# Dense hop products with their operands swapped, float32r hop tables in two parts, and a reload without a split, in a two-layer graph kernel

## What is computed

```python
h = jnp.maximum(_layernorm(x, axis=-1), 0.0)
m_data, m_ctrl = h[src] @ W_data.T + b_data, h[src] @ W_control.T + b_control
msg = jnp.where((edge_types == 0)[:, None], m_data, m_ctrl)
x = x + relu(segment_sum(msg, dst) + (h @ W_self.T + b_self))
h = jnp.maximum(_layernorm(x, axis=-1), 0.0)
norm = deg_inv_sqrt[row] * deg_inv_sqrt[col]
y, out = h, h
for _ in range(2):
    y = segment_sum(y[row] * norm[:, None], col)
    out = out + y
x = x + out / 3
```

## Time and profile before

| | before |
|---|---|
| median of three runs | 3998.82 us |
| lowest, highest | 3994.66, 3999.19 us |
| span of the profiled execution (first to last instruction) | 3997.9 us |
| granted TensorE clock, mean over the span | 0.945 of 2.4 GHz |
| PE busy | 3405.9 us (85%) |
| PE weight loads busy | 2729.2 us (68%) |
| POOL busy | 2879.8 us (72%) |
| ACT busy | 2329.7 us (58%) |
| DVE busy | 2186.3 us (55%) |
| HBM traffic | 424.48 MB read, 142.99 MB written |

### The profile page before, as it was taken

How to read it: one execution, slowest core, us unless ns; L and a number is a source line. 1 busy time by engine, 2 the same in 40 slices (tenths; PEclk the granted TensorE clock), 3 DMA queues, 4 the chain that set the end, 5 groups by cost and what they waited for, 6 DMA issues and landing times.

```text
span 3997.9 us, 62254 instructions
## 1 busy us (share of the span) xinstructions
PE 3405.9 (85%) x23420; PEld 2729.2 (68%) x23420; DVE 2186.3 (55%) x3333; ACT 2329.7 (58%) x3075; POOL 2879.8 (72%) x3058
## 2 busy tenths in 40 slices
PE   7666777777777787777777899999998899999999
PEld 4344444444444444444444799999998899999999
DVE  7523888888888888888888422222222222222222
ACT  4001444444444444444444688888887788888887
POOL 2677777777777777777777577777776477777775
PEclk9788998999999999999999999999999999999999
DMA  6222333333333334333333566666666666666665
GB/s 194 85 61 61 109 119 121 113 109 110 126 109 110 114 110 128 110 109 125 110 115 112 170 179 187 192 192 187 189 189 184 179 179 176 187 182 181 179 184 145
DMA packets 367268, 571.77 MB, mean 143 GB/s; under 512 B 66678, under 2 KB 308225, under 8 KB 359283
## 3 DMA queue, kind: packets, MB, share of 16 engines
q1 hardware_dynamic: 270435, 370.74, 29.6%
q0 software_dynamic: 95664, 196.60, 19.2%
q10 hardware_dynamic: 864, 0.39, 0.0%
HBM read 424.48 MB, written 142.99 MB: 142 GB/s over the span
## 4 chain that ended last, share of the span: by engine, by line
PE 44%; POOL 38%; issue 13%; DVE 2%; DMA 2%; ACT 1%; SPq 0%; DVEq 0%; POOLq 0%; ACTq 0%
POOL rows L874 38%; PE wide L1175 34%; PE sums_bank L1091 7%; PE wide L1056 1%; ACT strip_ring L1011 1%; DMA stage<-hop_table 1%; DMA rows<-typed_table,index 0%; PE turned_bank L1126 0%; DVE big L1214 0%; DVE rows L1254 0%; DVE stage L1512 0%; POOL stage L914 0%; PE wide L1135 0%; DMA stage<-strips 0%; DMA big<-in_x 0%
## 5 line engine op out<-in xcount | busy, mean ns | idle before, releaser
L874 POOL DMA_INDIRECT rows<-typed_table,index x1661 | 1589.0, 957 | 506.0 <-issue 505.0
L874 POOL DMA_INDIRECT rows<-hop_table,index x1306 | 1251.9, 959 | 481.4 <-issue 394.9
L1011 ACT CAST strip_ring<-stage 128x1792 fp32r<-128x1792 uint8 x840 | 1409.2, 1687 | 285.3 <-PE wide L1175 279.2
L1175 PE MATMUL wide<-table_parts,strip_ring 128*128 128x256 f32 x11760 | 1461.0, 285 | 35.7 <-ACT strip_ring L1011 35.7
L1175 PEld LDWEIGHTS wide<-table_parts,strip_ring 128*128 128x128 f32 x11760 | 1431.3, 193 | 38.0 <-ACT strip_ring L1011 17.5
L1002 ACT CAST stage<-wide 128x392 uint8<-128x392 f32 x1920 | 790.3, 502 | 983.9 <-PE wide L1135 982.6
L1126 PE MATMUL turned_bank<-all_twos 128*128 128x512 bf16 x3328 | 1112.0, 394 | 0.0
L1091 PE MATMUL sums_bank<-rows,hot 128*128 128x129 f32 (+1 forms) x5934 | 801.2, 292 | 287.0 <-DMA rows<-typed_table,index 272.6
L1091 PEld LDWEIGHTS sums_bank<-rows,hot 128*128 128x128 f32 x5934 | 764.4, 206 | 337.8 <-issue 304.0
L1512 DVE TENSOR_TENSOR stage<-count_up,stage 128x1568 bf16<-128x1568 f32 x480 | 855.4, 1782 | 0.0
L1135 PE MATMUL wide<-stage 128*128 128x392 bf16 x1920 | 652.6, 340 | 221.8 <-DVE stage L1512 220.0
(11 more groups left out here) (141 smaller groups left out, 669.5 us busy)
## 6 DMA issues: line engine op xcount, KB each, us to landing
stage<-strips SPq DMA_DIRECT2D x840, 224.0 KB
strips<-stage SPq DMA_DIRECT2D x60, 1568.0 KB
rows<-typed_table,index POOLq DMA_INDIRECT x1661
rows<-hop_table,index POOLq DMA_INDIRECT x1306
resid<-xin SPq DMA_DIRECT2D x50, 256.0 KB, 3.0
hop_table<-scaled SPq DMA_DIRECT2D x50, 256.0 KB, 3.8
xin<-resid SPq DMA_DIRECT2D x50, 256.0 KB
typed_table<-rows SPq DMA_DIRECT2D x49, 256.0 KB, 2.1
```

Of the source, the lines that this page charges most:

```text
L874: pool.indirect_dma_start(out=rows[:, o % RING, c, 0:P], out_offset=None, in_=tables[k], in_offset=bass.IndirectOffsetOnAxis(ap=index[:, c ...
L1011: act.copy(strip_ring[:, number % STRIP_RING], counts_ring[place]).then_inc(strip_cast, 1)
L1175: last = pe.matmul(wide[:, nth % 4, 0:PARTS * P], strip_ring[:, number % STRIP_RING, b - first, :], table_parts[:, b, :, :].rearrange("p n ...
```

## The change

The parts:

- **Dense product.** The table part of a block becomes the stationary operand, and the counts of four tiles (a whole batch) the moving one, 512 columns. A step is now 4 blocks x 4 tiles; the product comes out transposed (features by nodes), is copied from PSUM in one piece per batch (`read_batch`) and turned back by four transposes (`turn_batch`). A hop has 375 steps (15 batches x 25 pieces; the last piece of a batch has 2 blocks). A count load covers two steps: 128 partitions x 4 tiles x 1024 bytes, ring of 3.
- **Hop tables in two parts.** `finish` of pass 0 and of hop 1 makes a high part (ACT) and a low part (DVE); both are stored, so that a table row is 1024 bytes. The gathers of the hops fetch rows of 1024 bytes as float32r; `sum_rows` has 256 columns in float32r, and `add_group` adds high and low one after the other. The gathers' ring has 3 places in the hops (4 in pass 0).
- **Reload.** A DMA moves the 1024-byte rows straight into `table_parts`; `part_high`, `part_low` and their ring are gone. 14 pieces as before, 917 KB each in place of 459 KB.
- **Lead.** One batch, 4 steps a slot (24 steps before hop 1, 22 before hop 2), in place of three tiles, 3 steps a slot (18 and 15).

```diff
-STEP_BLOCKS = 14
-COUNT_RING = 7
+STEP_BLOCKS = 4
+LOAD_STEPS = 2
+COUNT_RING = 3
-LEAD_TILES = 3
-LEAD_AT_ONCE = 3
+LEAD_BATCHES = 1
+LEAD_AT_ONCE = 4
...
-        rows = sbuf("rows", [RING, CHUNKS, TILE])
-        hot = sbuf("hot", [HOT_RING, CHUNKS, P])
+        hop_rows = sbuf("hop_rows", [HOP_RING, CHUNKS, PARTS * P], F32R)
+        hop_hot = sbuf("hop_hot", [HOT_RING, CHUNKS, P], F32R)
...
             def store_nodes(n, k, s, even):
-                    sp.wait_ge(scaled_ready, n + 1)
-                    sp.dma_start(of_batch(tables[k + 1], s), in_blocks(scaled[:, n % 2, :])).then_inc(table_stored[n % 2], 16)
+                    sp.wait_ge(low_ready, n + 1)
+                    for part, values in enumerate((high_of(k, s, even), low_of(n, k, s, even))):
+                        sp.dma_start(tables[k + 1][nodes, part * P:(part + 1) * P].rearrange("(b p) f -> p b f", p=P),
+                                     values.bitcast(F32)).then_inc(table_stored[n % 2], 16)
...
+                def reload(piece):
                     sp.wait_ge(strip_used, last_step_with(piece) + 1)
-                    if r >= RELOAD_RING:
-                        sp.wait_ge(reload_low, r - RELOAD_RING + 1)
-                    sp.dma_start(in_blocks(reloaded[r % RELOAD_RING], RELOAD_BLOCKS),
+                    sp.dma_start(table_parts[:, first:first + RELOAD_BLOCKS, :, :].rearrange("p b n f -> p b (n f)").bitcast(F32),
                                  tables[2][first * P:(first + RELOAD_BLOCKS) * P, :].rearrange("(b p) f -> p b f", p=P)
...
-                    pool.wait_ge(summed, o - RING + 1)
+                    pool.wait_ge(summed, o - RING + 1 if o < groups else max(groups, o - HOP_RING + 1))
...
             def finish(n, k, s, even):
+                    if n and not (k == 0 and even):
+                        act.wait_ge(table_stored[(n - 1) % 2], 32 * count_of(n, 2, (n - 1) % 2))
+                    act.copy(high_of(k, s, even), in_blocks(scaled[:, n % 2, 0:blocks * P], blocks)).then_inc(high_ready, 1)
...
                         for number in steps_at(k, i):
                             cast_counts(number)
+                        if finishing and k == 1:
+                            finish(finishing[0], k, finishing[1], True)
...
-                    for b in range(first, end):
-                        last = pe.matmul(wide[:, nth % 4, 0:PARTS * P], strip_ring[:, number % STRIP_RING, b - first, :],
-                                         table_parts[:, b, :, :].rearrange("p n f -> p (n f)"),
+                    for b in blocks:
+                        for part in range(PARTS):
+                            last = pe.matmul(wide[:, nth % 4, 0:BATCH].rearrange("p (t n) -> p t n", t=NODE_BLOCKS),
+                                             table_parts[:, b, part, :], strip_ring[:, number % STRIP_RING, :, b - blocks.start, :],
...
+                    for b in range(NODE_BLOCKS):
+                        last = pe.transpose(turned[:, b * P:(b + 1) * P], own_in[:, q % 2, b * P:(b + 1) * P], identity[:, :])
+                    last.then_inc(batch_turned, 1)
```

More of the change, by code:

```diff
@@ new lines, in parts_of_batch, with order_of_counts @@
+    def parts_of_batch(s):
+        return {block // (STEP_BLOCKS * LOAD_STEPS) for block in range(s * NODE_BLOCKS, min((s + 1) * NODE_BLOCKS, real_blocks))}
+    last_of_pass = [{total - 1}, {total - 1, DENSE_BATCHES - 1}]
+    def order_of_counts(k):
+        late = set().union(*(parts_of_batch(s) for s in last_of_pass[k - 1]))
+        lead = [(q, part) for q in range(LEAD_BATCHES) for part in range(loads) if part not in late]
+        order = lead + [(q, part) for q in range(LEAD_BATCHES) for part in sorted(late)]
+        order += [(q, part) for q in range(LEAD_BATCHES, DENSE_BATCHES) for part in range(loads)]
+        return sum(len(pieces_of_counts(part)) for _, part in lead), order
@@ new lines, in gnn_kernel @@
+    lead_steps, counts_orders = zip(*([(0, [])] + [order_of_counts(k) for k in range(1, HOPS + 1)]))
+    orders = [[(q, piece) for q, part in order for piece in pieces_of_counts(part)] for order in counts_orders]
+    assert all(len(orders[k]) == steps_per_hop and len(counts_orders[k]) == loads_per_hop for k in range(1, HOPS + 1))
+    counts_of_step = [n for k in range(1, HOPS + 1) for n, (_, part) in enumerate(counts_orders[k], (k - 1) * loads_per_hop)
+                      for _ in pieces_of_counts(part)]
@@ L164, in step_end @@
+    end_of_counts = [max(j for j, n in enumerate(counts_of_step) if n == m) for m in range(HOPS * loads_per_hop)]
     def step_end(k, i):
@@ L499, in table_need @@
         def table_need(k):
-            return [16 * count_of(k * total, 2, parity) for parity in range(2)]
+            return [32 * count_of(k * total, 2, parity) for parity in range(2)]
         def event_at(k, slot):
```

289 lines of the change are left out of this document (156 added, 133 removed).

## The result

The change makes the kernel a little faster, by less than half of what was forecast: 3975.51 us (median of 4 runs, 3974.17 to 3977.29) against 3999.01 for the kernel before (4 runs, 3994.66 to 4001.44) on the same chip, a ratio of 0.9939 with a 95% interval of 0.9927 to 0.995. That is 23.5 us gained for 50.8 forecast, and the time lies inside the range given (3930 to 4005). The profiled span is 3972.1 us against 3997.9.

The account below looks back on a forecast made before the run. PE bound the kernel at 10.17 us a slot, POOL close behind at 10.05. From 3997.9: +6.3 first edge, -7 and -3 gathers, -27 second edge, -19.4 tail, so -50: 3948 us, range 3930 to 4005.

Parts of the forecast that it names:

- Dense product: PE in the hops: half the matmuls, 512 columns each at 226 ns, 7.9 us a slot (7.5 to 8.4) for 8.39.
- sums: PE in the hops: eight float32r sums of 256 columns take 0.96 us a slot, for 1.78 in float32.
- ACT: Casts in the hops: 1.80 us per 2048 columns, 7.9 us a slot, hidden behind POOL.
- the gathers' own time: POOL in the hops: no growth with rows of 1024 bytes, 946 ns against 944 for 512.
- DMA engines: In the hops: 57 ns of one engine per 1024-byte row, 86% of a 10.05 us slot, so nothing waits.
- The two rivals on the engines and on POOL's time: In the hops: DMA engines become the bound, 4070 or 4219 us, 11%; POOL's time grows with the row, 4010, 3%.
- Clock: Rival in the hops: PE, idle about 1 us a slot, drops towards 1.2 GHz and holds POOL; some 4050 us, 2%.
- Tail: After POOL's last gather of hop 2: last sum and end come sooner, -19.4 us.
- Hop 1's gathers: POOL in hop 1: 1.256 us a gather, 10.05 us a slot, 820 us for 827.2, -7 us.
- Edge of pass 0: Before hop 1: cast behind eight casts for six +4.9, store +1.4; start at 2261.0 for 2254.7, +6.3 us.
- Edge of the hops: Between hops 1 and 2: PE's lag shrinks, then 24.5 us to restart; gap 33.5 us for 60.4, -27.
- the first rival: Reload stage before the second edge eats the gain: PE's lag of 45 us, 3988 to 3998 us, no change, 9%.

Follow-up runs that it names:

- the short lead: The changed kernel with 12 lead steps for 24, all behind the table's last store, the rest in the slots: 3950.44 us, ratio 0.9873.
- experiment 1: The changed kernel with its lead steps issued as 2, 2, 2, 6, 6, 6 in place of 4 a slot: 3960.51 us, ratio 0.9899.
- experiment 3: The changed kernel with seven of the eight gathers and sums of each group in both hops: 3794.94 us, ratio 0.948.

## Why the prediction was right in direction and wrong in size

*Dense product, sums, ACT, DVE, the gathers' own time:* right. 227 ns for 226, 0.96 us for 0.96, PE's slot about 8.8 for 9.0 where it is never idle (in the change itself it is busy for 92% of 10.05 us, at a granted clock of 0.97), 947 ns for a gather of twice the bytes, POOL the bound with no wait for PE.

*DMA engines:* right in kind, somewhat dear. 81% for 86, 52 ns for 57. The two rivals on the engines and on POOL's time are out: no wait of POOL in the hops.

*Clock:* PE's granted clock in hop 1 is 0.97 where it was 1.00, with PE idle 8% of the time; POOL wasn't held. The rival is out.

*Tail:* -21.2 us for -19.4.

*Hop 1's gathers, 5.9 us of the error.* The step was "I take 1.256 us, 10.05 us a slot, 820 us a hop". The price came from hop 2, and the prediction took 7 us off hop 1's 827.2 without a reason. The groups of line 874 and of line 913 in 800 us of each hop (count, busy, mean ns) say otherwise; the first two rows are before, the others after:

```profile
L874 POOL DMA_INDIRECT rows<-hop_table,index x632 | 608.4, 963 | 192.7 <-issue 192.0 <-PE sums_bank L1091 0.7
L874 POOL DMA_INDIRECT rows<-hop_table,index x636 | 607.2, 955 | 193.9 <-issue 192.1 <-PE sums_bank L1091 1.9
```

```profile
L913 POOL DMA_INDIRECT hop_rows<-hop_table,index x633 | 608.1, 961 | 192.9 <-issue 192.9
L913 POOL DMA_INDIRECT hop_rows<-hop_table,index x638 | 606.8, 951 | 194.4 <-issue 194.4
```

Hop 1's gathers are slower than hop 2's by 8 to 10 ns in the mean, in both kernels and with next to no wait for PE: POOL's own pace. All kernels with whole groups that didn't wait there took 825 to 829 us. The timelines show which gathers they are. In the change 34 of hop 1's 653 take over 1 us and 13 of hop 2's; their time above 0.95 us is 9.2 and 2.9 us, which is the difference of the hops. Every one of them runs beside an instruction of DVE, while none of the more than 370 gathers in each hop that have no DVE instruction beside them is long. Of the 30 beside the scaling of a batch (L1460), which only hop 1 has, 23 are long. So hop 1's longer gathers go with the work that DVE does there to finish a batch; whether they come from it isn't shown, as no experiment took that work away.

*Edge of pass 0, 9.8 us of the error.* The step that failed is "The table's store now waits for the low part (0.9 us) and is two DMAs (0.5): +1.4". The delay of the cast was seen (eight casts ahead for six) and was right: it comes at 2256.66, in the kernel before at 2250.79, 5.9 us sooner, of which 1.0 was there before the lead, so 4.9 as forecast. What was overlooked is SP: in the kernel before, the lead's count loads were all issued behind the last store, and in the change six of them stand ahead of it, each behind a cast. In SP's program of the change (cut):

```python
if leaving:
    store_nodes(leaving[0], k, leaving[1], True)
...
if i >= slots_of(k):
    load_counts_behind(steps_at(k, i))
```

Before, the second call stood under `if leaving == event_at(k, events[k][-1][0])`, that is, behind the last store only. The timeline of ACT and of SP's queue in the kernel before:

```profile
2250.79 0.41 ACT L982 CAST table_parts<-scaled 128x256 fp32r<-128x256 f32 x1 [0.83 <-DVE scaled L1404]
...
2250.85 0.51 SPq L732 DMA_DIRECT2D hop_table<-scaled  x1
2251.41 10.54 SPq L772 DMA_DIRECT2D stage<-strips  x11
```

In the change the low part was ready at 2257.60 and the store went out at 2265.64: 8.0 us. With the 1.0 us of pass 0 and 0.8 more than forecast between store and start this is the 9.8. With the lead 2, 2, 2, 6, 6, 6 the start moves 12.9 us forward, with none ahead 18.3. This shows the lead as the cause; casts and loads moved together in both, and only the timelines part them.

*Edge of the hops, 10.6 us.* The lag of PE was better than forecast, 5.9 us after POOL in place of 9. The step that failed is "nine lead steps of PE (16.3), a cast (1.8), then split and two stores (2.2) and their landing (4.2): 24.5 us". The lead's share came out (15.4 for eight casts, where 18.1 were forecast), and so did the rest behind it (6.5 for 6.4). Left out was that the last high part can't even start its turn until the two batches ahead have had the single place and their stores have landed, in a stretch where the reloads stand in SP's queue and fill the engines: 16.3 us. Less 3.1 for the lag and 2.7 for the lead this is the error of 10.6. Without the reloads the gap is 33.4, within 0.1 of the forecast, but that is luck: it is made of a lag of 4.1 and 29.3 behind it, for 9 and 24.5. The prediction had worked out the crowding (90 us of DMA work in 60) but let it fall on PE's counts alone, where it did little; it fell on the stores. So the first rival had the right stage, not the right path: a lag of 45 us was its condition, and the lag was 5.9.

In one sentence: the terms in the loop were near, except for hop 1's pace, while the edges were costed by ACT's order alone, without SP's and without the landing of the stores ahead.

What stays open: whether reloads that start only after the last store would shorten the gap of the short lead further (the short lead without reloads has no run either; with the lead of experiment 1 leaving them out gave 3945.96), whether two places for the high parts of full batches would, and what the swapped product gives without the wider rows. None of these was tried.

## What to carry to other kernels

When a faster engine takes a loop under the pace of another, the gain is only the lag that it had run up, and it is paid at the edges; there, follow the last store back on every queue that it passes (ACT's order, SP's order, the place in the buffer, the landing of the store before) rather than on the engine with the visible wait. Work that is brought forward to fill a gap stands ahead of what ends the gap. If the loop has slack now, it is cheaper to leave that work in the loop: half the lead, behind the last store, gave 25 us, none at all gave back 6 of them, as PE's lag then grew in the last slots of the hop, which the reloads crowd.

## What the runs showed of the hardware that was not expected

- An indirect DMA takes POOL 947 ns for 128 rows of 1024 bytes and 944 for 128 of 512, while a row's time on a DMA engine grows from 33.8 to 52 ns: twice the bytes for 1.54 times the time (in stretches where the engines are busy for 66% and 81%).
- A gather that takes over 1 us (the median is 947 ns) always had a DVE instruction beside it: 34 and 13 such gathers in the two hops of the change, 42 and 23 before, none among the 370 to 400 of a hop without one.
- With the engines full (nine tenths, some 345 GB/s between 3043 and 3120) the stores of the table wait in SP's queue as well as on the engines: an issue that takes 0.5 us at 3120.81 takes 2.2 there (3098.00 in the change), and a reload of 896 KB lands after 10.2 us.
- After 2.57 us of idle and 0.88 more, 32 dense matmuls took 10.27 us in place of 7.45; the granted clock was 0.71 in that stretch, part of it at 1.2 GHz and part at 2.4 (the window below, columns as in experiment 3). POOL's ring of three groups carried it over such slots.

```profile
2611.00:2621.00 10.00, 9.99 (x32) 8.02 (x33) 3.75 (x8) 8.72 (x5) 7.56 (x9) 0.71 0.86 255
```
